# A pre-norm decoder layer: self-attention with the values stationary, its masks added in the maximum pass, and its weights split once and streamed

## What is computed

```
h = x * rsqrt(mean(x * x) + EPS) * norm_w            # x is already layer-normalised
q, k, v = proj(w_q), proj(w_k), proj(w_v)            # 16 heads of 64
ll = einsum('bhnqd,bhnkd->bhnqk', qw, kw) * scale;  ll = where(tril, ll, -1e30)
scores = h @ scorer_w + scorer_b;  _, idx = top_k(scores, 128)
lg = einsum('bhsd,bhgd->bhsg', q, k[idx]) * scale;  lg = where(idx <= pos, lg, -1e30)
attn = softmax(concatenate([ll, lg]))                # a selected key counts twice
o = attn[:512] @ v + attn[512:] @ v[idx];  out = x + o @ w_out
```

## Time and profile before

| | us |
|---|---|
| median of 3 runs | 2419.62 (2413.27 to 2421.91) |
| profiled execution, span | 2414.0 |
| PE busy | 2241.6 (93%), 12029 instructions |
| PEld busy | 1682.4 (70%) |
| DVE busy | 1349.6 (56%) |
| ACT busy | 845.5 (35%) |
| POOL busy | 429.2 (18%) |

### The profile page before, as it was taken

How to read it: one execution, slowest core, us unless ns; L and a number is a source line. 1 busy time by engine, 2 the same in 40 slices (tenths; PEclk the granted TensorE clock), 3 DMA queues, 4 the chain that set the end, 5 groups by cost and what they waited for, 6 DMA issues and landing times. The chain is left out here.

```text
span 2414.0 us, 35686 instructions
## 1 busy us (share of the span) xinstructions
PE 2241.6 (93%) x12029; PEld 1682.4 (70%) x12029; DVE 1349.6 (56%) x3145; ACT 845.5 (35%) x1541; POOL 429.2 (18%) x669
## 2 busy tenths in 40 slices
PE   3999999999999999999999999996898888878899
PEld 3786777678678677767767767773787888865543
DVE  4574376177257437617725743661787878845500
ACT  3442344144144234314414423441644444413210
POOL 2100000010010000001001000002866666620000
PEclk9999999999999999999999999997988888858999
DMA  5000000100100000010010000002013211141000
...
DMA packets 46136, 80.23 MB, mean 33 GB/s; under 512 B 10067, under 2 KB 10067, under 8 KB 45448
## 3 DMA queue, kind: packets, MB, share of 16 engines
...
...
## 5 line engine op out<-in xcount | busy, mean ns | idle before, releaser
L405 ACT ACTIVATE probs<-s_bank,nmax 128x512 f32<-128x512 f32 (+3 forms) x512 | 249.4, 525 | 421.6 <-DVE nmax L530 294.3
L530 DVE TENSOR_REDUCE nmax<-s_bank 128x1 f32<-128x512 f32 (+2 forms) x384 | 185.3, 510 | 305.7 <-PE s_bank L665 302.0
L688 PE MATMUL o_bank<-vals,probs_t 128*128 128x65 f32 x2560 | 322.2, 269 | 0.0
L688 PEld LDWEIGHTS o_bank<-vals,probs_t 128*128 128x128 f32 x2560 | 311.0, 192 | 1.4 <-DVE probs_t L538 1.4
L712 PE MATMUL pj_bank<-w_o,o_t 128*128 128x512 f32 x512 | 223.5, 597 | 6.0 <-ACT o_t L413 6.0
L538 DVE COPY probs_t<-pt_bank 128x512 f32<-128x512 f32 x320 | 218.0, 681 | 3.6 <-PE pt_bank L673 3.6
L319 POOL TENSOR_TENSOR idle<-ones 128x4 f32<-128x4 f32 x41 | 8.1, 198 | 1065.7 <-DMA probs<-in_x 1063.7
L673 PE MATMUL pt_bank<-ident,probs 128*128 128x128 f32 x1280 | 194.1, 274 | 0.0
L712 PEld LDWEIGHTS pj_bank<-w_o,o_t 128*128 128x128 f32 x512 | 97.2, 191 | 127.6 <-issue 127.6
L664 PE MATMUL s_bank<-k_lo,q_both 64*128 64x512 f32 (+3 forms) x448 | 184.9, 413 | 0.0
L514 DVE SCALAR_TENSOR_TENSOR q_both<-pj_bank,q_both 64x512 fp32r<-64x512 f32 x128 | 88.2, 689 | 141.6 <-ACT q_both L392 138.9
(11 more groups left out here) (266 smaller groups left out, 4245.5 us busy)
## 6 DMA issues: line engine op xcount, KB each, us to landing
xb<-in_x SPq DMA_DIRECT2D x9, 1024.0 KB, 5.3
...
am<-in_L_ffn_attention_mask SPq DMA_DIRECT2D x8, 1024.0 KB, 5.2
...
o_t<-in_L_attn_w_v SPq DMA_DIRECT2D x2, 1024.0 KB, 9.5
```

The source lines that it names most:

```text
L405: ins = nc.scalar.activation(probs[:, i % 2, c0:c0 + nk], s_bank[i % 2][:, c0:c0 + nk], ACT.Exp, bias=nmax[:, i % 4, n:n + 1])
L530: ins = nc.vector.tensor_reduce(nmax[:, i % 4, n:n + 1], s_bank[i % 2][:, c0:c0 + nk], AX.X, ALU.max, negate=True)
L688: ins = nc.tensor.matmul(o_bank[slot][:, o0:o0 + VW], probs_t[:, i % 2, c0 + P * kt:c0 + P * kt + P], vals[:, kt, 2 * p + h, :], start=(kt ...
```

## The change

- Weights: a first slice of w_q and w_k (for pair 0) is split on its own; w_v is split and kept; the rest of w_q and w_k is split in eight pieces through two stage buffers and stored to a new tensor in HBM, `wqk_split`. From there SyncE's queue loads 1 MB for each head pair in each batch into one of two buffers (`load_pair`).
- Units: six a pair instead of five. Scores are two 128-row products, the low keys standing in a tile whose other head's rows are zero. They are formed negated, and no mask matmul follows.
- Mask: a table `bias` holds, for each query block, the causal mask plus -ln 2 for a selected key. VectorE adds it to the score bank, writes the sum to `probs` and takes the minimum in one operation. ScalarE's exponential reads and writes `probs` and gives the row's sum. GpSimd takes its reciprocal (a power of -1) and scales the row. For the table, the 0/-ln 2 of each token is transposed to a row (step tw) and GpSimd adds it (step bias), at the end of the batch before.
- Transposed scores are split too: high part on ScalarE (part of step t), low part on VectorE (step tl). A unit's transpose stands three units after its scores.
- Value product: two steps a pair. Each head's values, high beside low (128 columns), are the stationary operand, and the transposed scores are streamed, 512, 384, 256 and 128 columns, high and low. The bank's two halves are added by a ScalarE copy and a VectorE add into `o_t`, so the transposes of the outputs are gone.
- Order: four of the eight value projections stand before the units and four between them; the statistics stand right behind the first; x of the next batch is loaded once its scorer is done; queries and keys of pair 0 are projected at the end of the batch before; the ranks stand between the output blocks.

```diff
+    return ([(0, 3, 0, 512)], [(0, 2, 0, 384)], [(0, 1, 0, 256), (1, 1, 256, 256)],
+            [(0, 0, 0, 128), (1, 0, 128, 128)], [(1, 3, 0, 512)], [(1, 2, 0, 384)])[u]
...
+    plan = [("v", 0), ("stats", 0)] + [("v", i) for i in (1, 2, 3)] + [("qa", 1), ("qb", 1)]
+    for g in range(NU):
         p, u = divmod(g, UNITS)
...
+        if g >= LAG:
+            plan.append(("t", g - LAG))
+        plan.append(("s", g))
+        if g >= LAG:
+            plan.append(("tl", g - LAG))
+        if u == 2 and p:
+            plan.append(("pv", 2 * p - 2))
+        if u == 3 and p:
+            plan.append(("pv", 2 * p - 1))
+        if p + 1 < NPAIR and u < 2:
+            plan.append((("ka", "kb")[u], p + 1))
+        if p + 2 < NPAIR and u >= 4:
+            plan.append((("qa", "qb")[u - 4], p + 2))
+        if (p, u) in V_AT:
+            plan.append(("v", TT + V_AT.index((p, u))))
+        if g in HT_AT:
+            plan.append(("ht", HT_AT.index(g)))
+        if g == NU - 4:
             plan.append(("dot", 0))
-        if g == 18:
-            plan.append(("score", 0))
-        if g in RANK_AT:
-            plan.append(("rank", RANK_AT.index(g)))
-        if NU <= g < NU + DC:
-            plan.append(("ht", g - NU))
-        if g >= 9 and (g - 9) % UNITS == 0 and (g - 9) // UNITS < NPAIR - 1:
-            plan.append(("ot", (g - 9) // UNITS))
-    plan.append(("ot", NPAIR - 1))
-    plan += [("out", t) for t in range(TT)]
+        if g >= NU - 2:
+            plan.append((("qa", "qb")[g - NU + 2], NPAIR))
+    for k in range(LAG):
+        plan += [("t", NU - LAG + k), ("tl", NU - LAG + k)]
+        if k == 0:
+            plan.append(("ka", NPAIR))
+    plan += [("pv", 2 * NPAIR - 2), ("pv", 2 * NPAIR - 1), ("kb", NPAIR), ("out", 0), ("score", 0), ("out", 1),
+             ("rank", 0), ("rank", 1), ("out", 2), ("rank", 2), ("rank", 3), ("tw", 0), ("out", 3), ("bias", 0)]
     return plan
...
+                    if kind == "s":
+                        slot, n = i % 4, len(unit_blocks(i % UNITS))
+                        pl.wait_ge(p_ready, b * NU + i + 1)
+                        nc.gpsimd.tensor_tensor(rden[:, slot, 0:n], den[:, slot, 0:n], minus[:, 0:n],
+                                                ALU.pow).then_inc(rden_ready, 1)
+                        pl.wait_ge(rden_ready, b * NU + i + 1)
+                        nc.gpsimd.tensor_tensor(held_p[:, slot:slot + 1], ones[:, 0:1], ones[:, 0:1], ALU.mult)
+                        for n, (_, _, c0, nk) in enumerate(unit_blocks(i % UNITS)):
+                            ins = nc.gpsimd.tensor_scalar(probs[:, i % 3, c0:c0 + nk], probs[:, i % 3, c0:c0 + nk],
+                                                          rden[:, slot, n:n + 1], 1.0, ALU.mult, ALU.mult)
+                        ins.then_inc(norm_ready, 1)
...
                         for n, (_, _, c0, nk) in enumerate(unit_blocks(i % UNITS)):
-                            ins = nc.scalar.activation(probs[:, i % 2, c0:c0 + nk], s_bank[i % 2][:, c0:c0 + nk],
-                                                       ACT.Exp, bias=nmax[:, i % 4, n:n + 1])
+                            ins = nc.scalar.activation(probs[:, i % 3, c0:c0 + nk], probs[:, i % 3, c0:c0 + nk],
+                                                       ACT.Exp, bias=nmax[:, slot, n:n + 1], scale=-1.0,
+                                                       accum_out=den[:, slot, n:n + 1])
                         ins.then_inc(p_ready, 1)
+                    if kind == "t":
+                        slot, ready = pt(b, (kind, i))
+                        act.wait_ge(pt_ready, ready)
+                        dst, src = turned(pt_hi, i % UNITS, pt_bank[slot])
+                        nc.scalar.copy(dst, src).then_inc(pt_hi_ready, 1)
...
+                    if kind == "pv":
+
+                        p, h = divmod(i, 2)
+                        act.wait_ge(pv_ready, b * (2 * NPAIR) + i + 1)
+                        nc.scalar.copy(o_t[head_rows(h), p, :], o_bank[h][head_rows(1 - h), :]).then_inc(o_half, 1)
...
+            split(1)
+            biased(None, 0)
+            for i in range(2, len(W_ORDER)):
+                split(i)
...
+                    if kind == "v":
+                        hw, t = divmod(i, TT)
+                        slot, _ = pj(b, (kind, i))
+                        dv.wait_ge(v_hi, b * (2 * TT) + i + 1)
+                        nc.vector.tensor_tensor(vals[:, t, 4 * hw:4 * hw + 4, 1:3, :],
+                                                pj_bank[slot][:, :].rearrange("p (j h d) -> p j h d", h=2, d=HD),
+                                                vals[:, t, 4 * hw:4 * hw + 4, 0:4:3, :].bitcast(F32),
+                                                ALU.subtract).then_inc(v_lo, 1)
+                    if kind == "qb":
+                        queries_lo(b, i, b * NPAIR + i + 1)
+                    if kind == "kb":
+                        keys_lo(b, i, b * NPAIR + i + 1)
...
+                        nc.vector.memset(held_v[:, slot:slot + 1], 0.0)
+                        for n, (_, t, c0, nk) in enumerate(unit_blocks(i % UNITS)):
+                            ins = nc.vector.tensor_tensor_reduce(probs[:, i % 3, c0:c0 + nk], s_bank[i % 2][:, c0:c0 + nk],
+                                                                 bias[:, mask_cols(t)], 1.0, 3.0e38, ALU.add,
+                                                                 ALU.min, nmax[:, slot, n:n + 1])
                         ins.then_inc(max_ready, 1)
...
+                    if kind == "tl":
+                        slot, _ = pt(b, ("t", i))
+                        dv.wait_ge(pt_hi_ready, b * NU + i + 1)
+                        dst, src = turned(pt_lo, i % UNITS, pt_bank[slot])
+                        hi, _ = turned(pt_hi, i % UNITS, pt_bank[slot])
+                        nc.vector.tensor_tensor(dst, src, hi.bitcast(F32), ALU.subtract).then_inc(pt_lo_ready, 1)
...
+                        p, h = divmod(i, 2)
+                        rows = head_rows(h)
+                        dv.wait_ge(o_half, b * (2 * NPAIR) + i + 1)
+                        nc.vector.tensor_tensor(o_t[rows, p, :], o_bank[h][rows, :], o_t[rows, p, :],
+                                                ALU.add).then_inc(ot_ready, 1)
...
+            for i in range(2):
+                sp.wait_ge(staged[i], 64)
+            load_pair(1, 0)
+            for m in range(4, 8):
+                store_split(m)
+            for i in range(2):
+                sp.wait_ge(staged[i], 128)
+            sp.dma_start(w_o[:, :, :], w_out.rearrange("(c p) d -> p c d", p=P)).then_inc(small_in, 16)
...
+            def batch(b, source):
+                sp.wait_ge(score_ready, b + 1)
+                sp.dma_start(xb[:, :, :], x_rows[source]).then_inc(x_in, 16)
+                for n in range(2, NPAIR + 2):
+                    sp.wait_ge(k_hi_ready, b * NPAIR + (n - 2) + 1)
+                    load_pair(n, b)
+                results(b)
+
...
+                            queries = q_both[:, p % 2, h, P * t:P * t + P]
+                            nc.tensor.matmul(s_bank[slot][:, c0:c0 + nk], queries, k_twice[:, p % 2, h, 0:nk],
+                                             start=True, stop=False)
+                            ins = nc.tensor.matmul(s_bank[slot][:, c0:c0 + nk], queries, k_lo[:, p % 2, h, 0:nk],
                                                    start=False, stop=True)
...
+                            pe.wait_ge(ot_ready, b * (2 * NPAIR) + i - 1)
+                        for k in range(TT):
+                            for part in (pt_hi, pt_lo):
+                                ins = nc.tensor.matmul(
+                                    o_bank[h][:, P * k:S],
+                                    vals[:, k, p, 2 * h:2 * h + 2, :].rearrange("p s d -> p (s d)"),
+                                    part[:, h, 4 * k:3 * k + TT, :].rearrange("p t q -> p (t q)"),
+                                    start=(k == 0 and part is pt_hi), stop=(k == TT - 1 and part is pt_lo))
                         ins.then_inc(pv_ready, 1)
```

507 lines of the change are left out of this document (266 added, 241 removed).

## The result

The changed kernel took 2553.64 us (median of 4 runs, 2541.94 to 2557.34) beside 2419.99 us before: ratio 1.0562, 95% interval [1.0539, 1.0586]. Forecast were 2495 us, slower, with a range of 2350 to 2590. The direction and the range held; the size was 59 us short.

The account below looks back on a forecast made before the run. The prediction took a chain alternating between ScalarE and VectorE to bound self-attention: start 85 + 8 batches x 205.6 + 759.5 for the rest = 2489 us of span, with 5.6 to the median 2495 us; range 2350 to 2590.

Parts of the forecast that it names:

- What bounds the kernel: Self-attention: TensorE stops being the limit; ScalarE and VectorE alternate in one chain, 18.6 us a head pair beside 18.43 before.
- The pair of 18.6 us: Self-attention head pair without value projection: from its key copies to the next pair's, through ScalarE and VectorE in turn, 18.6 us.
- the read: ScalarE's accumulator read for the row sum after each exponential: 0.15 us taken, bounds 0 and 0.27.
- "maximum, exponential, output half, add" twice in a row: Units 2 and 3 in a pair's chain, VectorE and ScalarE alternating: from 3.86 to 9.55 us, before the second add.
- The value pairs, 3 x 19.25: Pairs 1 to 3 of a batch, with a value projection whose low part adds 0.6 us to the chain: 19.25 each.
- rival C: TensorE's clock falls to 0.84 with its waits; start, output and value pairs grow by 8; batch 214, 2560 us; chance 0.16.
- The start, 85: Before the eight batches: weight pieces split through two stage buffers, stores and loads; 85 us, bounds 65 and 100.
- The 5.6 us from span to median: Added to the summed span of 2489 us, as the median before lay 5.6 above the profiled span.
- The two new waits: Each batch: 1.6 us at its start for the second value's low part, 4.7 before the last output block for ranks.
- Rival A: Self-attention: TensorE stays the bound, the three-unit lag hiding the chain; batch 164.6, time 2167 us; chance 0.10.
- Rival B: Pair's chain shorter: no accumulator read, perhaps overlapping copies; pair 16.8 to 17.4, time 2380 to 2420 us; chance 0.24.
- Rival D: Narrow split products cost as much as wide ones, or streamed weights come late (2655 us); chance 0.03.

Follow-up runs that it names:

- e2: Changed kernel with VectorE's low parts of keys and queries moved behind the next maximum; 2385.1 us, ratio 0.9875 to the kernel before.
- e3: Changed kernel with the value projection ahead of the pair's second value product, in the three pairs that have one; 2493.4 us.
- e9_best: e8_all with the statistics back behind the first value projection and the next x loaded once the scorer has read the last; 2255.6 us.
- e4_filler: Changed kernel plus twelve thrown-away products ahead of the second value product in pairs 1 to 3; 2514.1 us.
- e11: Changed kernel with output halves and adds later, and twelve thrown-away products ahead of the second value product in pairs 1 to 5; 2470.5 us.
- e8_all: Changed kernel with output halves, adds and low parts later, value projection ahead of the second value product, statistics and ranks moved; 2307.8 us.

## Why the prediction was right, and where it fell short

- **What bounds the kernel** was right: TensorE stops being the limit and the loop takes turns. e2 shows it with a pure reordering (-168 us). TensorE's idle share was forecast near 30%; it is 19% in a pair (3.4 of 17.9 us), since its work at half clock fills the rest.
- **The pair of 18.6 us** was 17.9; the read of 0.10 instead of 0.15 is 0.4 of the 0.7. The exponentials from memory took 394 ns at 128 columns and 724 at 512 in the mean, as priced, beside 368 and 689 from a score bank. What the Trainium skill says there (ScalarE: Activation LUTs, Step-by-step: what each stage is for), that the engine sits closer to PSUM, agrees with that in direction; its advice is on an operation's destination, whereas here only the source moved. That the step "maximum, exponential, output half, add" twice in a row is the way from unit 2 to unit 4 was half the truth. Beside it runs unit 5's low part, second value product, scores of unit 4 and 5, equally long only because it runs at 1.2 GHz. The number was right, the list of what would shorten it was not.
- **The value pairs, 3 x 19.25**, are the term that failed: 20.8 to 21.9. The prediction had the clock as rival C and priced it (batch 214, 2560), which is close to what came (212.6, 2553.6; in part by luck, as it stands on pairs of 18.6 that took 17.9), but gave it 0.16 and left it out of its own sum. What happened is forecast and rival C together: they were no alternatives, as the clock falls in the waits that the chain makes. Its grounds for doubt, that the stretches between waits are dense, don't hold: one wait of 3.4 us a pair is followed by eight slow products. Of the prediction's own signs of being wrong, a clock well under 1 is the one that came. The rule of the Trainium skill named there (TensorE: Matmul & The Clock Gate, HAM oscillation) agrees with this trace: 0.84 granted from 372.5 to 383 us, 1.00 in e3's pair.
- **The start, 85**: measured 97, within its bounds (65 to 100). The rounds of two pieces took 9 to 12 us and not 6.4, as each piece waits until its own stage buffer is stored, and x came behind the output weights at 102.9 and not 89. The 5.6 us from span to median had no ground in the runs: an execution's time lies 1.7 above its own span (2557.34 beside 2555.6), and the rest is which execution was profiled.
- **The two new waits** are there. TensorE's waits for the second value's low part are 56.6 us in 9, of which 30.4 and 14.8 in the start: 11.4 in 7, 1.6 each (forecast 1.6). Its waits for the ranks are 45.8 us in 9, one of 10.7 in the start: 4.4 a batch (forecast 4.7). Removing both brought 6.8 us at the border of a batch (forecast 1.6 + 4.7).
- **Rival A** (2167, nothing in the way) fell: 84 of 100 us busy. With the order mended, e9_best comes within 90 us of it (176.2 us a batch, A 164.6); what keeps the rest wasn't tried. A's sum is itself not worked out in full: its 42.8 us beside the start and the pairs is given without terms, where the output's own term is 33.3. **Rival B** (shorter chain): its copies don't overlap and the read isn't free; it fell. **Rival D**: value products of 512, 384, 256 and 128 columns come 0.23, 0.17, 0.12 and 0.06 us after one another at full clock; narrow is cheap.

## What to carry to other kernels

When a change takes work from the engine that was full, count next the longest way through the program orders of the other engines; a loop with no full engine was cured here by order (11.6%, with not one operation removed), and two branches may be equally long, so that each edit alone shows nothing. If the formerly full engine now waits, even for 1.7 us (e9_best), price its following work at the low clock too in the forecast itself, and put its own independent work into the wait. Work that an engine does once a batch has to be counted against every loop it stands in, GpSimd's too.

## What the runs showed of the chip beyond that

- Throwing work at TensorE made the kernel 39 us faster (e4_filler), because the products behind it then ran at 2.4 GHz.
- Waits of 3.4 to 4.4 us were followed by products at 1.2 GHz in the pairs and output blocks shown here, waits of 0.6 to 1.2 us (e3, e9, e11) were not. Between them it went both ways: 1.68 in e9_best was followed by 0.89 over the pair, 2.10 in e2_lo_later by 1.00 in one pair and 0.89 in another. So the length of one wait doesn't decide it.
- ScalarE's accumulator read shows as 0.19 us but costs about 0.1, as the next exponential begins before it ends.
- GpSimd's power took 0.55 us on one column, 0.71 on two and 1.02 on four (e8_all), so its price is mostly not that of the elements.
